# The routed layer with 64 experts: row lists per expert pair, and the rows moved beside the experts

## The reference

```
for each of T = 2048 tokens, n = layernorm(x):
    s = n @ gate_w + gate_b                     # 64 scores
    take the 3 largest; gates = softmax of the 3
    pos = how many earlier tokens chose the same expert
    kept = pos < 64                             # the expert's capacity
for each expert e, on its at most 64 rows:
    y = gelu(rows @ w1[e] + b1[e]) @ w2[e] + b2[e]   # 128 -> 512 -> 128
x += tanh(g) * sum over the 3 choices of kept * gate * y
```

## Time and profile before

| | |
|---|---|
| time, median of 3 runs | 1963.48 us (1958.14 to 1964.47) |
| the profiled execution | 1958.99 us, span 1957.2 us |
| busy: PE, PEld, DVE, ACT, POOL | 1568.4, 728.2, 888.8, 677.1, 417.4 us |
| granted TensorE clock over the span | 0.867 |
| DMA | 72.16 MB, mean 37 GB/s |

### The profile page before, as it was taken

How to read it: one execution, slowest core, us unless ns; L and a number is a source line. 1 busy time by engine, 2 the same in 40 slices (tenths; PEclk the granted TensorE clock), 3 DMA queues, 4 the chain that set the end, 5 groups by cost and what they waited for, 6 DMA issues and landing times. The chain is left out here.

```text
span 1957.2 us, 20649 instructions
## 1 busy us (share of the span) xinstructions
PE 1568.4 (80%) x7386; PEld 728.2 (37%) x7386; DVE 888.8 (45%) x1477; ACT 677.1 (35%) x1096; POOL 417.4 (21%) x395
## 2 busy tenths in 40 slices
PE   5877686108990469999999999996999997675997
PEld 2223222108990223333333333333655654223443
DVE  3757562501131355665665665643333333523433
ACT  3454243002110235555554554643222223243111
POOL 0012010260006214453553544440000000010000
PEclk8888696555595689999999999998999998796999
DMA  8102104214522200000000000002000000001000
GB/s 267 72 0 64 37 1 156 82 47 151 194 64 65 69 0 1 1 1 1 1 1 1 1 1 1 1 1 92 1 0 0 0 0 27 0 1 53 0 0 22
DMA packets 29837, 72.16 MB, mean 37 GB/s; under 512 B 5838, under 2 KB 17102, under 8 KB 28622
## 3 DMA queue, kind: packets, MB, share of 16 engines
q1 hardware_dynamic: 26684, 64.81, 9.9%
q0 software_dynamic: 3072, 6.30, 1.1%
HBM read 64.80 MB, written 8.39 MB: 37 GB/s over the span
## 5 line engine op out<-in xcount | busy, mean ns | idle before, releaser
L1591 ACT ACTIVATE a_prob<-a_TP 128x512 f32<-128x512 f32 x256 | 138.9, 595 | 188.1 <-PE a_TP L1414 187.9
L1688 DVE TENSOR_REDUCE a_lat<-a_SP 128x2 f32<-128x1024 f32 x128 | 156.0, 1219 | 52.4 <-PE a_SP L1383 52.4
L1410 PE MATMUL a_TP<-a_qn,a_kn 64*128 64x512 f32 x512 | 148.9, 645 | 3.0 <-ACT a_prob L1591 3.0
L710 DVE TENSOR_TENSOR f_hv<-f_gl,f_VP 128x512 f32<-128x512 f32 (+1 forms) x96 | 65.8, 686 | 162.2 <-ACT f_gl L676 162.2
L2347 POOL TENSOR_TENSOR a_on<-a_osb,a_rden 128x512 f32<-128x512 f32 x9 | 11.4, 1268 | 556.2 <-ACT a_osb L2111 556.2
L676 ACT ACTIVATE f_gl<-f_HP 128x512 f32<-128x512 f32 (+1 forms) x96 | 57.2, 595 | 199.3 <-PE f_VP L658 199.3
L1425 PE MATMUL a_O<-a_prob,a_V 128*64 128x512 f32 x512 | 122.6, 599 | 0.2 <-ACT a_prob L1591 0.2
L645 PEld LDWEIGHTS f_YP<-f_W,f_hv 128*128 128x128 f32 (+1 forms) x768 | 100.5, 192 | 47.9 <-issue 43.7
L656 PE MATMUL f_HP<-xn,f_W 128*128 (+1 forms) x192 | 103.2, 620 | 16.4 <-PEq L560 11.0
L1803 POOL TENSOR_TENSOR a_acc<-a_prob 128x512 f32<-128x512 f32 x64 | 79.6, 1264 | 160.0 <-ACT a_prob L1591 160.0
L2182 DVE TENSOR_REDUCE a_nm<-a_A 128x8 bf16<-128x616 f32 x96 | 76.6, 798 | 69.5 <-PE a_A L1962 69.4
(11 more groups left out here) (393 smaller groups left out, 2842.1 us busy)
## 6 DMA issues: line engine op xcount, KB each, us to landing
ring_w<-in_F_w SPq DMA_DIRECT2D x64, 512.0 KB, 8.3
a_maskT<-in_maskT SPq DMA_DIRECT2D x1, 2304.0 KB
a_biasT<-in_biasT SPq DMA_DIRECT2D x1, 2304.0 KB
f_b<-in_F_b SPq DMA_DIRECT2D x1, 2048.0 KB
f_xs<-dispatched SPq DMA_DIRECT2D x4, 512.0 KB, 5.9
expert_out<-f_xs SPq DMA_DIRECT2D x2, 1024.0 KB, 7.4
a_biasQ<-in_biasQ SPq DMA_DIRECT2D x1, 1848.0 KB, 7.5
f_W<-in_F_w SPq DMA_DIRECT2D x1, 1536.0 KB
```

The source lines that it names most:

```text
L1410: nc.tensor.matmul(TP[0:n, h, :], keys(h), qn[half(h), r % 4, :], start=True, stop=False)
L1591: nc.scalar.activation(prob[0:n, 2 * k + h, :], TP[0:n, h, :], ACT.Exp, bias=rowneg[0:n, b:b + 1] if k == 0 else 0.0).then_inc(p_ready, 1)
L1688: nc.vector.tensor_reduce(lat[:, g % 2, 2 * u:2 * u + 2], SP[:, :, :], AX.X, ALU.max, negate=True).then_inc(s_used, 1)
```

## The change

The layer is rewritten around lists by expert pair.

- Normalisation, routing, ranks and lists are one block that works by batches of 512 tokens. GpSimd makes the one-hot sums and the running counts; ScalarE stores the turned token rows to DRAM (`xrows`).
- TensorE builds for each pair a list of 128 row numbers, by products of position one-hots weighted with the row number (`lw`) and expert one-hots (`hot`). VectorE makes from it a source index and a destination index.
- There are no scatters of all rows ahead of the pairs. GpSimd fetches a pair's 128 rows with one indirect DMA, the first six (AHEAD) before the block ends, the others beside the pairs; TensorE turns them just before their pair, one transpose each (`turn`), and ScalarE keeps them.
- A pair's results are sent with one indirect DMA to the DRAM buffer `expert_rows`, laid out by choice and token. It is zeroed at the start of the kernel, 3 MB where the old buffer had 2 MB.
- The loop over the pairs is written out, in the order up(n), turn(n+2), down(n-1) for all 32.
- The ring holds 12 slots during the routing and 16 during the pairs.
- The last block reads the results with 12 plain DMAs; ScalarE does the first of three gate multiplications.

No dense product whose result isn't read stands ahead of the pairs, before or after. The core of the diff:

```diff
-    SLOTS, EARLY = 16, 8
+    EARLY, ROUTED, SLOTS = 8, 12, 16
...
+    def extend(self, c, ctx, upto):
+        self.slots += [self.buffers(c, ctx, i) for i in range(len(self.slots), upto)]
...
+    def load(self, sp, pair):
+
+        slot = pair % self.SLOTS
...
+            sp.dma_start(dst[:, :], src[pair, :, :]).then_inc(self.loaded[slot], 16)
...
+    c.xrows = c.nc.dram_tensor("token_rows", [T, D], F32, kind="Internal").ap()
+    c.yrows = c.nc.dram_tensor("expert_rows", [3 * T + 32 * P, D], F32, kind="Internal").ap()
...
-        sp.dma_start(c.disp[0:4096, :].rearrange("(p q) d -> p (q d)", p=P), c.dram["zeros"])\
+        sp.dma_start(c.yrows[0:2 * T, :].rearrange("(p q) d -> p (q d)", p=P), c.dram["zeros"])\
+            .then_inc(c.rows_zeroed, 16)
+        sp.dma_start(c.yrows[2 * T:3 * T, :].rearrange("(p q) d -> p (q d)", p=P), c.dram["zeros"][:, 0:TILES * D])\
             .then_inc(c.rows_zeroed, 16)
...
+            def fetch(n):
+                nc.gpsimd.indirect_dma_start(
+                    out=xs[:, n % FETCH, :], out_offset=None, in_=c.xrows[:, :],
+                    in_offset=bass.IndirectOffsetOnAxis(ap=src[:, n:n + 1], axis=0)).then_inc(rows_in[n % FETCH], 16)
...
+                        def variance(b):
+                            pe.wait_ge(squared, b + 1)
...
+                        def lists(b):
+                            pe.wait_ge(weighted, (b + 1) * K * QT)
+                            for k in range(K):
+                                for q in range(QT):
+                                    at = (b, k, q)
+                                    for h in range(2):
+                                        mm = nc.tensor.matmul(LIST[CAP * h:CAP * h + CAP, :], lw[:, b % 2, k, q, :],
+                                                              hot[:, b, k, q, h:E:2], start=at == (0, 0, 0),
+                                                              stop=at == (B - 1, K - 1, QT - 1))
+                            mm.then_inc(listed, 1)
...
+                        for b in range(B):
+                            nc.tensor.matmul(CEN[:, b, :], c.center[:, :], c.xT[:, tokens(b)], start=True,
+                                             stop=True).then_inc(centred, 1)
+                        variance(0)
+                        variance(1)
+                        pe.wait_ge(r_loaded, 32)
+                        route(0)
+                        variance(2)
+                        route(1)
+                        variance(3)
+                        pe.wait_ge(upper_cast, 1)
+                        route(2)
+                        count(0)
+                        route(3)
+                        count(1)
+                        pe.wait_ge(logged, 3)
+                        lists(0)
+                        count(2)
+                        lists(1)
+                        count(3)
+                        lists(2)
+                        lists(3)
...
+                        def rank(b):
...
+                            nc.vector.tensor_tensor(
+                                prod[:, :, :, :], hot[:, b, :, :, :],
+                                ranks(b).rearrange("p (k t e) -> p k t e", k=1, t=QT).broadcast_to([P, K, QT, E]),
+                                ALU.mult).then_inc(multiplied, 1)
+                            dve.wait_ge(multiplied, b + 1)
+                            nc.vector.tensor_reduce(pos[:, b, :, :], prod[:, :, :, :], AX.X, ALU.add)\
...
+                            for k in range(K):
+                                for q in range(QT):
+                                    t = b * QT + q
+                                    nc.vector.tensor_scalar(lw[:, b % 2, k, q, :], c.iota[:, :],
+                                                            pos[:, b, k, q:q + 1], dst1[:, k, t:t + 1],
+                                                            ALU.is_equal, ALU.mult).then_inc(weighted, 1)
...
+                        step(nc.vector.tensor_copy(lst[:, :], LIST))
...
+                        step(nc.vector.tensor_scalar(late[:, 0, :], lst[:, :], float(T) + 0.5, float(T), ALU.is_ge,
+                                                     ALU.mult))
...
+                        step(nc.vector.tensor_scalar(gone[:, :], lst[:, :], 0.5, None, ALU.is_lt))
+                        step(nc.vector.tensor_tensor(late[:, 0, :], late[:, 0, :], late[:, 1, :], ALU.add))
+                        step(nc.vector.scalar_tensor_tensor(out=late[:, 0, :], in0=lst[:, :], scalar=-1.0,
+                                                            in1=late[:, 0, :], op0=ALU.add, op1=ALU.subtract))
+                        step(nc.vector.tensor_scalar(src[:, :], late[:, 0, :], 0.0, None, ALU.max))
...
+                    def _(pool):
+                        nc.gpsimd.memset(run[:, 0, :], 0.0).then_inc(run_made, 1)
+                        for b in range(B):
+                            pool.wait_ge(hot_made, b + 1)
+                            nc.gpsimd.tensor_tensor(pair_hot[:, :, :], hot[:, b, 0, :, :], hot[:, b, 1, :, :],
+                                                    ALU.add).then_inc(sum2, 1)
+                            pool.wait_ge(sum2, b + 1)
+                            nc.gpsimd.tensor_tensor(OH[:, b * QT:(b + 1) * QT, :], pair_hot[:, :, :],
+                                                    hot[:, b, 2, :, :], ALU.add).then_inc(oh_made, 1)
+                            pool.wait_ge(oh_made, b + 1)
+                            for q in range(QT):
+                                t = b * QT + q
+                                if t + 1 < TILES:
+                                    pool.wait_ge(run_made, t + 1)
+                                    nc.gpsimd.tensor_tensor(run[:, t + 1, :], run[:, t, :], OH[:, t, :],
+                                                            ALU.add).then_inc(run_made, 1)
+                        pool.wait_ge(tok_stored, 16 * B)
+                        pool.wait_ge(list_steps, 8)
+                        for n in range(AHEAD):
+                            fetch(n)
...
+                    for n in range(ring.ROUTED, ring.SLOTS):
+                        ring.load(sp, n)
+                    for n in range(ring.SLOTS, PAIRS):
+                        sp.wait_ge(y_ready, n - ring.SLOTS + 1)
+                        ring.load(sp, n)
+
+                @block.gpsimd
+                def _(pool):
+                    def send(n):
+                        pool.wait_ge(y_kept, n + 1)
+                        nc.gpsimd.indirect_dma_start(
+                            out=c.yrows[:, :], out_offset=bass.IndirectOffsetOnAxis(ap=dest[:, n:n + 1], axis=0),
+                            in_=ys[:, n % SEND, :], in_offset=None).then_inc(rows_out[n % SEND], 16)
+
+                    pool.wait_ge(c.rows_zeroed, 32)
+                    for n in range(AHEAD, PAIRS + AHEAD):
+                        if n < PAIRS:
+                            if n >= FETCH:
+                                pool.wait_ge(rows_turned, n - FETCH + 1)
+                            fetch(n)
+                        if n - AHEAD >= 2:
+                            send(n - AHEAD - 2)
+                    send(PAIRS - 2)
+                    send(PAIRS - 1)
...
-                @block.gpsimd
...
-                    for t in range(TILES):
-                        for k in range(TOPK):
-                            i = k * TILES + t
-                            nc.gpsimd.indirect_dma_start(
-                                out=c.disp[:, :], out_offset=bass.IndirectOffsetOnAxis(ap=slot_in[:, i:i + 1], axis=0),
-                                in_=xtok[:, t, :], in_offset=None).then_inc(scattered, 16)
-                    pool.wait_ge(scattered, 16 * TILES * TOPK)
...
-            @block.sync
-            def _(sp):
-                for i in range(4):
-                    sp.dma_start(xs[:, 8 * i:8 * i + 8, :], c.disp[1024 * i:1024 * (i + 1), :]
-                                 .rearrange("(q p) d -> p q d", p=P)).then_inc(rows[i], 16)
...
-                with sp.Fori(0, PAIRS // R - 1) as it:
-                    for i in range(R):
-                        sp.wait_ge(y_ready, it * R + i + 1)
-                        ring.load(sp, i, (it + 1) * R + i)
-                    store(it)
...
-            @block.tensor
-            def _(pe):
-                with pe.Fori(0, PAIRS // R) as it:
...
+                    def turn(n):
+                        pe.wait_ge(rows_in[n % FETCH], 16 * (n // FETCH + 1))
+                        if n >= 2:
+                            pe.wait_ge(xs_ready, n - 1)
+                        nc.tensor.transpose(XT[:, n % 2, 0:P], xs[:, n % FETCH, :],
+                                            c.ident[:, :]).then_inc(rows_turned, 1)
+
+                    def up(n):
+                        slot = n % ring.SLOTS
+                        pe.wait_ge(ring.loaded[slot], 32 * (n // ring.SLOTS + 1))
+                        pe.wait_ge(xs_ready, n + 1)
```

(51 more changed lines are left out.)

512 lines of the change are left out of this document (279 added, 233 removed).

## The result

The changed kernel takes 1823.97 us (median of 4 runs, 1821.47 to 1832.82), the kernel before in the same rounds 1960.81 us (4 runs, 1957.93 to 1964.47): a ratio of 0.931, with a 95% interval of 0.927 to 0.934. It is faster by 137 us where I forecast 66.4 (a time of 1895), and outside my range. The profiled execution, 1832.82 us with a span of 1831.0, is the slowest of the four.

What follows compares the result with a forecast made beforehand. GpSimd's indirect-DMA issue bounded two 66 us stretches, VectorE and TensorE others of the 341 us layer. Savings 66.2 - 48.8 + 49.0 = 66.4 us took 1958.99 to 1892.6; with the median's offset the forecast was 1895, range 1835 to 1912.

Steps and rivals of the forecast that it cites:

- part B: First up-product to last kept row, the 32 pairs: 185.3 us instead of 136.5 at the low clock, 48.8 more.
- The first rival: The clock rises inside the pairs: 1809 us if early (chance 0.13), 1810 to 1890 if in mid stage (0.07).
- its second form: The clock rises in mid stage of the pairs, 2.7 us gained per pair after it, 1810 to 1890 us; chance 0.07.
- A: Layer start to first up-product (normalisation, routing, lists, first fetches): 66.0 us instead of 132.2, 66.2 less.
- C: Last kept row to last update of xT: 23.6 us instead of 72.6, 49.0 less.
- the 4.5 named beside it: Offset of the median of the runs shown above the profiled execution, 4.5 us, named beside the 1892.6.
- the bounds: Open prices of lists, seams, turn, loads and VectorE's weightings, said to give 1873 to 1912 us at the low clock.
- The turn: One transpose added to each pair: 0.30 us each at the low clock, 9.6 in all, bounds -2.9 to +7.7.
- The lists: TensorE's list products before the pairs: 4.7 us a block, 22 for four with counts and handovers; bound -7.4.
- The seams: Block changes after GpSimd's issues, before the pairs and before the final loads: 4.0 us each, bounds -3.6 to +1.7.
- The combine: After the last send and seam: twelve plain loads at 13.3 us, then sums, transposes and update at 5.0.
- GpSimd was no bound: In the pairs: GpSimd's send and fetch take 2.52 us against 5.8; the rival, GpSimd bound and slower, had 0.03.

Runs made afterwards that it cites:

- e6: The kernel of e1 (no turns in pairs 2 to 31) reordered to up, up, down, down in every two pairs; 1811.29 us.
- e1: The changed kernel without the turns of pairs 2 to 31 and their copies; 1884.08 us.
- e3: The changed kernel with each turn moved into the middle of the up group, between its two experts; 1893.26 us.
- e12: The changed kernel with the list products reordered, all twelve of one column half before the other instead of in turn; 1855.82 us.
- e7: The changed kernel with VectorE's sums of block b+1 placed ahead of the update of xT with block b; 1808.03 us, one run.
- e15: The changed kernel with two row buffers for the sends instead of four; 1817.92 us, one run.
- e2: The kernel before, hardware loop unchanged, with one unread transpose directly ahead of each down group; 1930.48 us.
- e10: The changed kernel with the order up, down, turn in each pair instead of up, turn, down; 1819.56 us.
- e5: The kernel of e4 with the Gelu table loaded at the end of routing and two unread products after the first two turns; 1813.40 us.
- e4: The changed kernel with twelve unread products of 512 columns behind the last lists; 1813.00 us.
- e18: The changed kernel itself timed a third time, unedited; 1823.72 us, ratio 0.929 to the kernel before.
- e11: The changed kernel itself timed and profiled a second time, unedited; 1821.64 us, ratio 0.928 to the kernel before.

## Why the prediction was wrong

**The step that failed** is the start of part B, "At the low clock sixteen took 452.68 to 540.28, 87.6 us; thirty-two take 175.2": it put all 32 pairs at the low clock, because "up, turn, down repeats for all 32 pairs" and the old loop's seam was gone. I had the parts of the right answer. The old rise was read as two dense groups back to back (e6 shows it), the transposes of the earlier trace rows raised the clock by themselves, and the text says that the turn "works towards a rise". Then I weighed the turn by its length, "a sixth or less" of a down group (its row is 0.42 us beside 1.98), and gave the rise 0.20. The runs show that this much is enough: without it no rise before the last two down groups, 175.5 us on (e1), with it at the down group a rise in every profiled execution, after 9 to 90 us (eight with the turn ahead, one behind it, and in the old loop after 20.5), and with it four up-products away none (e3). The small piece had to be judged by the place where it stands, not by its share of the pair.

The first rival happened, in its second form, a rise in mid stage, to which I gave 0.07. The time of 1809 assumed a rise at once; with one after 9 to 38 us in the profiled executions the medians are 1818 to 1824. By that form 25 pairs at 2.7 us less give 1892.6 - 67.5 = 1825 for the profiled execution; it took 1832.8, with A 5.6 shorter, B 0.9 longer, C 4.9 longer and 7.2 more behind the layer. The other terms, by the prediction's steps:
- **Had the clock stayed low, the time would have come out right, in part by luck.** e3 is the nearest case, with the turn elsewhere: A, B and C of 61.8, 179.6 and 28.7 against 66.0, 185.3 and 23.6, and 1893.3 us against 1895. A and B were 9.9 too long together, and C too short by 5.1 and the rest by 4.3 made up for it.
- **Two sums were off by 2 to 3 us.** 1892.6 and the 4.5 named beside it give 1897, not 1895; the bounds add up to -22.2 and +13.7, so that the upper end is 1909, not 1912, and the lower one has them all on one side. Neither matters beside 70 us.
- **The turn** costs 0.22 us at the low clock (5.73 against e1's 5.51; predicted 0.30) and 0.12 at the high one (3.07 against 2.95 in the earlier trace rows; predicted 0.15).
- **The lists.** 4.7 us a block was mis-sized: it is 2.77, because the column halves overlap (e12). VectorE is the bound, as the lower bound had it, but not at four ranks of 4.0: the weightings take 0.23 each and not 0.17, so a rank takes 4.65 (354.57 to 359.23 between the starts of two). Lists end at 366.8; I had 371.4 and 364 as its bound.
- **The seams**, 4.0 each, were 2.8 and 5.2, both inside the bounds.
- **The combine** was mis-sized, 28.5 against 23.6. I priced the loads (13.3) and a tail of 5.0. The loads are not the bound: each block takes VectorE 4.18 us (515.71 to the next sums at 519.89), 2.31 for the sums, 0.75 for the update, and a wait for the transposes between them. I had put the order of VectorE's own work at nothing.
- **GpSimd** was no bound: 0.97 to 1.00 us a send and 0.94 to 1.15 a fetch (e7), with the DMA engines 0.96 busy from 384 to 450 us. A send, landed after 2.2 us in the earlier trace rows, now lands after 5.2 in the median and 9.8 at the most (e7). The prediction gave keep 23 us for it; at the high clock it is 11.7 (four pairs less the way to the send), still enough; the 5.6 of e15 was not, yet cost the pairs only 2.4.
- **What lies behind the layer** I left unchanged; it took 1302.7 us in the changed kernel's profile and 1295.4 in that of before, with the same instructions and more of them at the low clock. Single executions differ by 10 us there.

**On the rules weighed.** "TensorE: Matmul & The Clock Gate" of the Trainium skill, "Why this matters for your kernels", says that keeping the engine busy raises the clock. e1 and e3 disagree, at 0.50 with TensorE busy for 175.9 of 176 us and for 179.3 of 180. The same page of the Trainium skill, Part 4 ("PE-mode transpose"), says that transposes do not count as the engine being busy; e1 against the changed kernel, with e2 and e10, shows that one transpose in each pair, here of float32, decides the level.

## What to carry to other kernels

Where the profile shows TensorE without idle time at the low clock, try another order before paying for anything else: here two down groups back to back, or one transpose directly at each down group, raised it. Unread products in an idle stretch ahead helped too: the clock stayed up when they reached nearly up to the first real one (e5), and fell and came back in e4, whose time was the same. When a stage may get twice as fast, count every wait in it at that pace too, and then whether it is on the path: 35 us of waits for landings cost 2.4. A stall that comes and goes between chips is no evidence for an edit: run both versions on one chip. And move an engine's own waits behind work it could do first, since a block's end cost 3.0 us here and the waits in the middle of VectorE's queue 3.7.

## What was unexpected of the hardware

- The instant of the rise differs between executions of the same order of work: 9.2 (four times), 15.1, 38.0, 83.7 and 89.5 us after the first up-product. That moves the pairs from 102.9 to 137.5 us (e12), and to 140.8 in e18's longest execution, more than any edit but those of e1, e3 and e6. What decides it isn't settled.
- Products of a 64-column stationary operand into alternating column halves take 0.058 us a record, in the other order 0.102, at the same low clock (2.77 and 4.90 us for 48).
- With the DMA engines 0.96 busy, an indirect DMA costs GpSimd hardly more (0.97 to 1.00 us a send, against 0.96 at 0.15), and only its landing moves, from 2.2 to 5.2 us in the median (e7).
- In eight profiles (the seven on two of five chips, and the changed kernel's first) semaphore increments of TensorE came late, by 2.4 us in the pair shown of e11 and by 3.7 at the most in the changed kernel's first profile (470.5 to 474.2), and pairs with them in seven of the eight; all of this at the high clock, none in the same profiles at the low one. The other chips show none at either level.
- A block's end behind GpSimd's indirect DMAs cost 2.8 and 5.2 us; with no block's end the next engine followed after 1.4.
